# Reordering the first and second scores in the third layer's attention

## The reference

```python
q = (x @ Wq).reshape(B, T, nh, hd).transpose(0, 2, 1, 3)      # B=4, T=1024, nh=16, hd=8
...
attn = jnp.einsum('bhqd,bhkd->bhqk', q, k) / jnp.sqrt(jnp.float32(hd))
bias = slopes[:, None] * (jnp.arange(T, dtype=jnp.float32) - (BLOCK_SIZE - 1))
attn = attn + bias[None, :, None, :]
masked = jnp.where(causal[None, None], attn.astype(jnp.float32), jnp.finfo(jnp.float32).min)
probs = jax.nn.softmax(masked, axis=-1)
out = jnp.einsum('bhqk,bhkd->bhqd', probs, v)
```

## Time and profile before

| what | value |
|---|---|
| median of 3 runs | 2721.7 us (2717.99 to 2723.5) |
| profiled execution, its own time | 2723.18 us |
| profiled execution, span | 2721.5 us |
| mean granted TensorE clock over the span | 0.924 |
| this stage, first to last matmul | 1722.9 to 2254.0 us of the span |
| one iteration, with TensorE at its full clock | 30.98 us |

### The profile page before, as it was taken

The page is one execution under the profiler, slowest core; times in us unless marked ns, Lnnn a source line. Parts: engine busy times, 40 slices in busy tenths (PEclk is TensorE's granted clock), DMA queues, the critical chain, the costliest instruction groups (busy, mean ns, idle before and its releaser), DMA issues. The chain is left out here.

```text
span 2721.5 us, 49199 instructions
## 1 busy us (share of the span) xinstructions
PE 2361.2 (87%) x16668; PEld 1392.6 (51%) x16668; DVE 1720.8 (63%) x4914; ACT 1321.8 (49%) x2678; POOL 881.4 (32%) x1044
## 2 busy tenths in 40 slices
PE   4589998998999999999999397899999995888965
PEld 2356766995666676666666265322222223233322
DVE  7646663222566666665666745678878854699994
ACT  2146664443666666665666433156666673321213
POOL 1036664442556733332333213011111110133340
PEclk9679998997999999999999678699999997989978
DMA  5211113103011100000000016111111100000001
GB/s 153 101 52 32 31 31 85 32 25 123 17 31 17 31 2 17 2 17 3 2 2 2 3 44 193 52 32 32 32 33 35 42 6 32 0 0 0 0 0 31
DMA packets 77830, 93.67 MB, mean 34 GB/s; under 512 B 10065, under 2 KB 56162, under 8 KB 75922
## 3 DMA queue, kind: packets, MB, share of 16 engines
q1 hardware_dynamic: 64098, 77.23, 9.4%
q0 software_dynamic: 13488, 13.28, 2.4%
HBM read 54.55 MB, written 35.53 MB: 33 GB/s over the span
## 5 line engine op out<-in xcount | busy, mean ns | idle before, releaser
L957 ACT ACTIVATE WA<-a_E 128x1024 f32<-128x1024 f32 (+3 forms) x384 | 301.3, 815 | 162.1 <-PE a_E L896 123.6
L613 ACT COPY a1b_PT<-a1b_T 128x512 f32<-128x512 f32 (+3 forms) x288 | 153.7, 534 | 206.8 <-PE a1b_T L524 206.8
L434 POOL TENSOR_SCALAR XR<-XR,a1b_rinv 128x384 f32<-128x384 f32 (+1 forms) x192 | 162.0, 856 | 268.3 <-DVE a1b_rinv L686 268.1
L514 PE MATMUL a1b_S<-a1b_Kf,a1b_Qf 64*128 64x512 f32 (+3 forms) x1164 | 243.0, 522 | 0.0
L539 PE MATMUL a1b_O<-a1b_PT,WA 128*64 128x128 f32 x3456 | 225.8, 277 | 14.8 <-ACT WA L617 14.8
L681 DVE COPY a1b_PT<-a1b_T 128x128 f32<-128x128 f32 (+3 forms) x288 | 140.5, 488 | 154.0 <-PE a1b_T L524 153.9
L872 PE MATMUL a_S<-a_KS,a_QS 54*128 54x512 bf16 (+3 forms) x768 | 205.3, 355 | 32.7 <-DVE a_mx L993 19.3
L539 PEld LDWEIGHTS a1b_O<-a1b_PT,WA 128*64 128x64 f32 x3456 | 186.0, 137 | 81.8 <-ACT a1b_PT L613 39.7
L434 POOL TENSOR_SCALAR WA<-WA,a1b_rinv 128x128 f32<-128x128 f32 (+1 forms) x194 | 121.5, 639 | 214.5 <-DVE a1b_rinv L686 214.5
L872 PEld LDWEIGHTS a_S<-a_KS,a_QS 54*128 54x128 bf16 x768 | 60.4, 94 | 236.9 <-DVE a_mx L993 132.0
L604 ACT ACTIVATE XR<-XR,a1b_nmax 128x384 f32<-128x384 f32 (+1 forms) x192 | 168.1, 881 | 3.1
(11 more groups left out here) (402 smaller groups left out, 5135.2 us busy)
## 6 DMA issues: line engine op xcount, KB each, us to landing
WA<-in_w SPq DMA_DIRECT2D x8, 1024.0 KB, 9.4
a_QS<-qstack SPq DMA_DIRECT2D x32, 216.0 KB
a_KS<-kstack SPq DMA_DIRECT2D x32, 216.0 KB
a1b_tb<-tab SPq DMA_DIRECT2D x12, 512.0 KB, 4.6
qstack<-f_parts SPq DMA_DIRECT2D x24, 256.0 KB, 4.0
kstack<-f_parts SPq DMA_DIRECT2D x24, 256.0 KB, 4.2
f_slots<-f1r_zrows SPq DMA_DIRECT2D x9, 516.0 KB, 6.5
f1t_xs<-f_slots SPq DMA_DIRECT2D x9, 516.0 KB, 6.0
```

Of the source, the lines that this page charges most:

```text
L434: pool.tensor_scalar(soft(i0, u), soft(i0, u), rinv[:, n:n + 1], 1.0, ALU.mult, ALU.mult).then_inc(n_sb, 1)
L514: pe.matmul(pS[k % NB][:, 0:hi - lo], Qf[half, b0 % 2, i0 * P:(i0 + 1) * P], Kf[half, b0 % 2, lo:hi], start=True, stop=True).then_inc(s_ps, 1)
L613: act.copy(PT[:, i % 2 * HG + u, lo:hi], pT[0][:, 0:hi - lo]).then_inc(t_sb_a, 1)
L957: act.activation(PT[:, q % NP, :, off:CH], pE[q % 2][:, :, off:CH], ACT.Exp).then_inc(e_sb, 1)
```

## The change

Two edits. First, `sunits` is reordered: before, the twelve first-score units stand as (3,0), (2,0), (1,0), (0,0), (4,0), (5,0), (6,0), (7,0), (7,1), (6,1), (5,1), (4,1); after, as (0,0), (1,0), (2,0), (4,0), (3,0), (5,0), (6,0), (4,1), (7,0), (7,1), (6,1), (5,1). Second, `second` issues both pairs at the start of a step, the matmuls of both pairs before the mask matmuls of both, where before the first scores of one pair stood between them. The numbers of instructions, their shapes and their semaphores stay.

```diff
-    sunits = [(i, 0) for i in (3, 2, 1, 0, 4, 5, 6, 7)] + [(i, 1) for i in (7, 6, 5, 4)]
+    sunits = [(0, 0), (1, 0), (2, 0), (4, 0), (3, 0), (5, 0), (6, 0), (4, 1), (7, 0), (7, 1), (6, 1), (5, 1)]
...
-            def second(it, q):
-
-                c, j = eunits[q // 2]
+            def second(it, n):
+
+                c, j = eunits[n]
                 s = it % NS
-                if q == 0:
+                if n == 0:
                     pe.wait_ge(mrow_in[s], (it // NS + 1) * ROW_IN)
-                pe.wait_ge(e_sb, it * EQ + q + 1)
                 off = max(0, j * P - c * CH)
                 diag = j >= c * CT
-                for half in range(2):
-                    ins = pe.matmul(pE[q % 2][:, half, off:CH], KS[s][ROW[half], q % 2, j * P:(j + 1) * P],
-                                    QS[s][ROW[half], q % 2, c * CH + off:(c + 1) * CH], start=True, stop=not diag)
+                for pair in range(2):
+                    pe.wait_ge(e_sb, it * EQ + 2 * n + pair + 1)
+                    for half in range(2):
+                        ins = pe.matmul(pE[pair][:, half, off:CH], KS[s][ROW[half], pair, j * P:(j + 1) * P],
+                                        QS[s][ROW[half], pair, c * CH + off:(c + 1) * CH], start=True, stop=not diag)
+                    if not diag:
+                        ins.then_inc(e_ps, 1)
                 if diag:
-                    for half in range(2):
-                        ins = pe.matmul(pE[q % 2][:, half, off:off + P], identb[:, :], maskk[:, :], start=False, stop=True)
-                ins.then_inc(e_ps, 1)
+                    for pair in range(2):
+                        for half in range(2):
+                            ins = pe.matmul(pE[pair][:, half, off:off + P], identb[:, :], maskk[:, :], start=False, stop=True)
+                        ins.then_inc(e_ps, 1)
...
                 for n in range(STEPS):
-                    second(it, 2 * n)
+                    second(it, n)
                     if ahead(it, n):
                         first(*ahead(it, n), 0)
-                    second(it, 2 * n + 1)
                     if n:
                         weigh(it, n - 1)
```

## The result

The changed kernel takes 2752.3 us (median of 4 runs, 2741.4 to 2769.2) where the kernel before took 2722.5 beside it: 1.011 times as long, 95% interval 1.009 to 1.014. Run again later it took 2755.9 (2747.8 to 2766.6), ratio 1.011 (1.007 to 1.016). It is slower by 30 us, and the forecast said 2714. It is also more uneven: 28 us between the fastest and the slowest of four runs, where 24 runs of the kernel before lie within 17, and the runs order themselves by the mean granted clock of TensorE: 2741.4 at 0.912, 2749.4 at 0.908, 2755.2 at 0.907, 2769.2 at 0.902.

What follows compares the result with a forecast made beforehand. It took one in-order TensorE queue serving two customers with small buffers to bound the stage. 11.6 us saved in iterations, less 1.8 at the ends and 2.3 for clock falls, gave 7.5 off 2721.7: 2714 us, range 2702 to 2727.

Steps and rivals of the forecast that it cites:

- What bounds the kernel: Touched stage: no engine full; one in-order TensorE queue serves two customers with small buffers; VectorE works 25.74 of 30.98 us.
- The walk: One touched-stage iteration carried through step by step at full-clock prices: 30.12 us against 30.98, 0.86 saved per iteration.
- step 8: Step of the touched stage's iteration, put at 2.64 us: ScalarE idle about 0.7, then two exponentials.
- step 0: Step of the iteration, put at 3.12 us: ScalarE's copy stands between two exponentials, waiting for values behind first scores.
- step 4: Longest step of the iteration, put at 3.2 us: VectorE late, first scores wait for slots; past 3.3 meant forecast wrong.
- Rivals 2 and 3: Waits come back elsewhere, iteration stays 30.98, 2721 us, chance 0.24; VectorE stays fed, 1.5 or more saved, 2702, chance 0.14.
- The ends of the stage: Last steps lack first scores to cover ScalarE's idle time; with the first two steps of iteration 15, 1.8 us lost.
- The first iteration: Touched stage's first iteration, at half clock: no change expected, possibly off by 3 us either way.
- the sum's 9.8 of gain: Whole touched stage: 11.6 us saved over 13.5 full-clock iterations, less 1.8 lost, before 2.3 for clock falls.
- The hole on ScalarE: ScalarE idle about 0.7 us before its first exponential in 8 of 12 steps; covered where VectorE sets the step.
- The clock: TensorE's granted clock falls to half after thin work: two or three falls in place of one, 2.3 us more.
- the first rival: Clock falls in nearly every iteration, in step 4: 1.54 us for each of 13 more, 2732 us, chance 0.14.

Runs made afterwards that it cites:

- the kernel before, filled: Kernel before the change plus useless TensorE matmuls: second scores in steps 1 and 5, first scores in steps 0 and 4; 2718.0 us, ratio 0.9981.

## Why the prediction was wrong

The prediction gave 2714, with 2702 to 2727, and 0.57 for faster; the kernel is slower by 1.1%, outside the range, on the side that had 0.18.

**What bounds the kernel** held: no engine is full, and in the full-clock iterations the work of VectorE was 25.7 to 26.1 of 30 to 31 us.

**The walk** held. It gave 30.12 us per iteration and a saving of 0.86; at full clock the new order takes 29.95 and saves 1.03. Nor is that a sum of errors that cancel: in the iteration of the changed kernel without a fall, from one start of pair 1's second scores to the next, step 8 took the 2.64 that it gave, step 0 3.25 where it gave 3.12, step 4 3.42 where it gave 3.2, and no step is off by more than about 0.3. Step 4 is past the 3.3 that it named as a sign of being wrong, at no cost to the sum. Rivals 2 and 3 are out as far as the schedule goes: neither 30.98 nor 29.4.

**The ends of the stage** were about right. Behind the last cast the new order takes 35.7 us with the clock at full where the kernel before, filled, takes 33.3: 2.4 lost against the 1.8 of the sum. The first iteration, put at nothing within 3, took 32.6 instead of 34.5 in the two profiles. At full clock the sum's 9.8 of gain thus stand against 14 x 1.03 less 2.4, 12.0 us.

**The hole on ScalarE** was priced as uncovered at full clock in step 8; moving the masks gave back only 0.05 per iteration. The step by itself was right, but it was not on the path of the iteration.

**The clock** is the step that failed, as a term of the sum: "two or three in place of one: 2.3 us more". What was mis-sized is how often and how long, not the price: a short fall costs 31.44 - 29.95 = 1.5 us, against the 1.54 of the earlier trace rows, and the one of double length 32.71 - 29.95 = 2.8. In the profiled execution, which was the mildest, the clock fell thirteen times in the thirteen iterations from the second cast to the last but one, four times at double length, and they took 413.7 us where thirteen at full clock take 389.4: 24 us lost. In the other profile of the changed kernel, of a run of 2762.2, they took 432.5: 43 us lost, 34.13 - 29.95 = 4.2 in each iteration where the falls have settled. The mechanism, the place (step 4) and the price of a short fall were in the first rival, and its time of 2732 was still 20 short, since it allowed one short fall per iteration and left out step 0, although the walk gave that step 3.12 us too. The Trainium skill, page "TensorE: Matmul & The Clock Gate", section "A second HAM failure mode: psum-queue depth-cycling", says what the prediction cites from it, that small idles between groups of matmuls can make the clock go up and down. The trace agrees: the longest idle time ahead of a matmul between the second cast and the last is 0.62 us, and the clock fell in every iteration. Whether the cycling through banks has a part in it, no run here shows.

Why it had 0.14 only: I counted the falls as if each iteration threw a die, from one fall in 14 iterations. That one fall, as I read it now, said something else: the thinnest stretch of the old order was just thin enough, in one of 14 iterations. The new order thinned out TensorE's work around steps 0 and 4, which were the thin places already (dear first scores, narrow values, a copy to wait for), and where the falls settled they came twice per iteration. That reading is argued, not shown; what the filling shows is that with the thin places filled the schedule pays what the walk promised, and that the same work in steps 8 and 9 leaves a fall in nearly every iteration.

The saving that was promised is thus real, and is overpaid: 14 x 1.03 = 14 us gained, and a stage that is 12.8 longer in the profiled execution, so 27 us went to the clock and the stage's ends in the mildest run, 24 of them between the casts.

## What to carry to other kernels

A reordering that evens out the waits of two slow engines can thin out the work of the fast one; before trusting a walk made with full-clock prices, look for the longest stretches in which TensorE would mostly wait, and take one fall of the clock in the old trace as a possible sign that there is no margin, not as a rate. To tell a bad schedule from a bad clock, add useless matmuls where TensorE idles, and the same ones elsewhere as a control: here the first made the kernel 43 to 48 us faster, the second 15. Here moving the masks into TensorE's waits gave 40 us with no work added, and filling what was left another 17.

## What the runs showed of the hardware

The falls are not scattered. In a stage of equal iterations they settled in patterns that repeat: three iterations of 32.7, 31.4 and 31.4 us in one execution of the changed kernel, 34.13 nine times on end in another, 33.2 and 31.7 in turn with the filling in steps 8 and 9. The unaltered changed kernel took 2741 to 2769 us; the two executions of it that have profiles, 2741.4 and 2762.2, had different patterns.

The stages behind the touched one, which no kernel altered, took 466 to 469 us in seven profiles, with a granted clock of 0.86 to 0.88 there, and 472 to 474 in the other seven, with 0.85. Each kernel was profiled once, the changed one twice (473.2 both times), so that the sort is independent of the edit is not shown. It is 5 us in code that no edit touches, and a reason to take the effect from the stage's casts rather than from the total.
